# First cross attention of a two-layer Perceiver block: each context turned by 32-row strips in one burst, placed around the scores

## The reference

```python
qp = einsum('bsi,id->bsd', q, kernel_q) + bias_q      # q = layernorm(x)
kp = einsum('bsi,id->bsd', k, kernel_k) + bias_k      # k = v = ctx_1024
vp = einsum('bsi,id->bsd', v, kernel_v) + bias_v
logits = einsum('bqd,bkd->bqk', qp, kp) / sqrt(512) + mask
attn = softmax(logits, axis=-1)
x = x + einsum('bqk,bkd->bqd', attn, vp)
```

## Time and profile before

| | us |
|---|---|
| median of 3 runs | 1436.13 (1433.35 to 1438.67) |
| the profiled execution | 1430.72 |
| its span, first to last instruction | 1429.4 |
| PE busy in the span | 1299.4 (91%) |
| DVE busy | 735.0 (51%) |
| ACT busy | 500.5 (35%) |
| mean granted clock of TensorE | 0.965 of full speed |

### The profile page before, as it was taken

The page is one execution under the profiler, slowest core; times in us unless marked ns, Lnnn a source line. Parts: engine busy times, 40 slices in busy tenths (PEclk is TensorE's granted clock), DMA queues, the critical chain, the costliest instruction groups (busy, mean ns, idle before and its releaser), DMA issues. The chain is left out here.

```text
span 1429.4 us, 25759 instructions
## 1 busy us (share of the span) xinstructions
PE 1299.4 (91%) x11133; PEld 947.5 (66%) x11133; DVE 735.0 (51%) x1501; ACT 500.5 (35%) x977; POOL 148.2 (10%) x153
## 2 busy tenths in 40 slices
PE   6999869989777899999999999998888688999998
PEld 5655554456435677777777777776677556888787
DVE  6367464535698355444555444555772455443442
ACT  3233224322103254544554454542433232221321
POOL 3400030044435000000000000000130100000000
PEclk9999989999988999999999999998999989999999
DMA  9134030000111011000011000002300010000100
GB/s 321 62 118 171 7 118 0 0 1 1 59 67 44 30 33 59 31 31 31 31 33 59 31 32 31 31 2 89 46 0 0 2 66 30 30 30 30 60 30 30
DMA packets 50757, 67.24 MB, mean 47 GB/s; under 512 B 18586, under 2 KB 19660, under 8 KB 50644
## 3 DMA queue, kind: packets, MB, share of 16 engines
q1 hardware_dynamic: 49136, 64.25, 13.8%
q10 hardware_dynamic: 1508, 1.35, 0.4%
HBM read 63.49 MB, written 2.10 MB: 46 GB/s over the span
## 5 line engine op out<-in xcount | busy, mean ns | idle before, releaser
L223 PE MATMUL bank<-xT,wT 128*128 128x512 f32 x576 | 138.9, 394 | 1.8 <-DVE wT L239 1.8
L223 PEld LDWEIGHTS bank<-xT,wT 128*128 128x128 f32 x576 | 108.4, 188 | 27.3 <-issue 2.4
L1560 ACT ACTIVATE W<-W,low 128x512 f32<-128x512 f32 x128 | 90.9, 712 | 64.4 <-DVE low L1479 64.4
L173 POOL TENSOR_TENSOR rstd<-rstd,half_pow 128x1 f32<-128x1 f32 x48 | 28.2, 595 | 757.2 <-DVE rstd L169 696.9
L1479 DVE CUSTOM_DVE_ANT_0 W<-bank,mask 128x512 f32<-128x512 f32 x128 | 80.8, 687 | 49.4 <-PE bank L1369 49.4
L223 PE MATMUL bank<-Wkv,ctxT 128*128 128x512 f32 x432 | 105.2, 396 | 0.0
L1472 DVE COPY XT<-bank 128x256 f32<-128x256 f32 x16 | 6.8, 425 | 191.2 <-PE bank L1390 191.2
L1556 ACT ACTIVATE K<-bank,vecT 128x512 f32<-128x512 f32 x64 | 44.0, 688 | 163.0 <-PE bank L223 163.0
L223 PEld LDWEIGHTS bank<-Wkv,ctxT 128*128 128x128 f32 x432 | 79.2, 188 | 28.9 <-issue 12.2
L223 PE MATMUL bank<-ctxT,Wkv 128*128 128x512 f32 x384 | 94.1, 399 | 3.2 <-DVE ctxT L240 3.2
L223 PE MATMUL bank<-woT,hR 128*128 128x512 f32 x384 | 94.8, 403 | 2.2 <-DVE hR L240 2.2
(11 more groups left out here) (346 smaller groups left out, 2129.3 us busy)
## 6 DMA issues: line engine op xcount, KB each, us to landing
W<-in_ctx_dram SPq DMA_DIRECT2D x26, 1024.0 KB, 5.3
XT<-in_ctx_dram SPq DMA_DIRECT2D x6, 1024.0 KB, 7.6
XT<-in_L_ffn_wi_dram SPq DMA_DIRECT2D x4, 1024.0 KB, 6.3
XT<-in_L_ffn_wo_dram SPq DMA_DIRECT2D x4, 1024.0 KB, 5.1
X<-in_x_dram SPq DMA_DIRECT2D x8, 256.0 KB, 10.9
W<-in_L_attn_Wv_dram SPq DMA_DIRECT2D x2, 1024.0 KB, 8.8
out_dram<-X SPq DMA_DIRECT2D x8, 256.0 KB, 2.9
W<-in_L_xattn_kernel_k_dram SPq DMA_DIRECT2D x1, 1024.0 KB, 7.8
```

The source lines that it names most:

```text
L173: pool.tensor_tensor(rstd[:, g:g + 1], rstd[:, g:g + 1], half_pow[:], ALU.pow).then_inc(rstd_ok.s, 1)
L223: ins = pe.matmul(dst, stationary(x, k), moving(y, k), start=(first and n == 0), stop=(last and n == len(passes) - 1), skip_group_check=True)
L1560: act.activation(PR[:, j, :], PR[:, j, :], ACT.Exp, bias=low[:, j:j + 1], scale=-1.0, accum_out=total[:, j:j + 1]).then_inc(expd.s, 1)
```

## The change

Three things change, all in the first cross attention. First, a context is turned by 64 transposes of 32 rows x 128 columns instead of 16 of 128 x 128: four of them stand side by side on the four 32-row strips of the array, and strip r writes bank r, so one burst fills all four banks. Second, since one burst takes all four banks, each burst waits for all the copies of the burst before it, and each engine empties two banks of each context (VectorE banks 0 and 1, ScalarE banks 2 and 3) with a destination in pieces of 32 columns. Third, the two bursts of the next pair move: that of b = 0 goes to the head of the step, ahead of the probabilities and the scores, that of b = 1 to the place between scores and attend; `result` moves one step later, and the loop gets one step more. The sync engine's list is not touched. `turn_strips` and `strip_of` are the second cross attention's own helpers, made common; there nothing else changes.

```diff
+        def turn_strips(first, src_of):
+            for t in range(4):
+                for k in range(4):
+                    for r in range(4):
+                        strip, to = slice(32 * r, 32 * r + 32), 32 * (4 * t + k)
+                        ins = pe.transpose(bank[:, first + r, to:to + 32], src_of(t, k)[strip, :], ident[strip, strip])
+            return ins
+
+        def strip_of(T, first, r):
+            dst = T.rearrange("f t (k s n) -> f (t k) s n", k=4, s=4)[:, :, r, :]
+            return dst, bank[:, first + r, :].rearrange("f (a n) -> f a n", n=32)
...
-            def context_pe(j, r):
-                c, b = r // 2, r % 2
-                if c == 0:
-                    pe.wait_ge(raw_in[j % 3][b].s, raw_in[j % 3][b](j // 3))
-                if 8 * j + r >= 4:
-                    pe.wait_ge((ctx_a if b else ctx_v).s, (ctx_a if b else ctx_v)((8 * j + r - 4) // 2))
...
-                for k in range(KT):
-                    ins = pe.transpose(bank[:, r % 4, k * P:(k + 1) * P], raws[j % 3][:, b, k, c * P:(c + 1) * P], ident[:])
-                ins.then_inc(ctx_pe.s, 1)
+            def context_pe(j, b):
+                pe.wait_ge(raw_in[j % 3][b].s, raw_in[j % 3][b](j // 3))
+                if 2 * j + b:
+                    pe.wait_ge(ctx_v.s, ctx_v(4 * j + 2 * b - 1))
+                    pe.wait_ge(ctx_a.s, ctx_a(4 * j + 2 * b - 1))
...
+                turn_strips(0, lambda c, k: raws[j % 3][:, b, k, c * P:(c + 1) * P]).then_inc(ctx_pe.s, 1)
...
-                for j in range(PAIRS + 1):
-                    if j:
+                pe.wait_ge(row_a.s, row_a(2))
+                for j in range(PAIRS + 2):
+                    if j + 1 < PAIRS:
+                        context_pe(j + 1, 0)
+                    if j >= 2:
+                        result_pe(j - 2)
+                    if 1 <= j <= PAIRS:
                         probs_pe(j - 1)
                     if j < PAIRS:
                         scores_pe(j)
-                    if j == 0:
-                        pe.wait_ge(row_a.s, row_a(2))
-                    if j:
+                    if j + 1 < PAIRS:
+                        context_pe(j + 1, 1)
+                    if 1 <= j <= PAIRS:
                         attend_pe(j - 1)
-                    if j + 1 < PAIRS:
-                        for r in range(8):
-                            context_pe(j + 1, r)
-                    if j:
-                        result_pe(j - 1)
...
-            def context_v(j, c):
-                dve.wait_ge(ctx_pe.s, ctx_pe(8 * j + 2 * c))
-                dve.tensor_copy(ctxT[j % 2][:, 0, c, :], bank[:, 2 * c % 4, :]).then_inc(ctx_v.s, 1)
+            def context_v(j, b, r):
+                dst, src = strip_of(ctxT[j % 2][:, b, :, :], 0, r)
+                dve.wait_ge(ctx_pe.s, ctx_pe(2 * j + b))
+                dve.tensor_copy(dst, src).then_inc(ctx_v.s, 1)
...
+                    if j + 1 < PAIRS:
+                        for r in range(2):
+                            context_v(j + 1, 0, r)
+                    if j >= 2:
+                        result_v(j - 2)
...
                     if j + 1 < PAIRS:
-                        for c in range(C):
-                            context_v(j + 1, c)
-                    if j:
-                        result_v(j - 1)
+                        for r in range(2):
+                            context_v(j + 1, 1, r)
```

More of the change, by code:

```diff
@@ L390, in query_pe @@
                         lambda h, c: XS[:, h, c, n * 512:(n + 1) * 512], C).then_inc(proj.s, 1)
[L392 to L398 removed]
+            def context_pe(j, b):
[3 more added lines that the diff above has]
+                    pe.wait_ge(ctx_a.s, ctx_a(4 * j + 2 * b - 1))
+                else:
                     pe.wait_ge(wt_v.s, wt_v(3 * C - 1))
[L400 to L402 removed]
+                turn_strips(0, lambda c, k: raws[j % 3][:, b, k, c * P:(c + 1) * P]).then_inc(ctx_pe.s, 1)
             def scores_pe(j):
@@ L406, in scores_pe @@
                     pe.wait_ge(masked.s, masked(j - 1))
+                pe.wait_ge(ctx_v.s, ctx_v(4 * j + 3))
+                pe.wait_ge(ctx_a.s, ctx_a(4 * j + 3))
                 for c in range(C):
-                    pe.wait_ge(ctx_v.s, ctx_v(4 * j + c))
-                    pe.wait_ge(ctx_a.s, ctx_a(4 * j + c))
                     for b in range(2):
@@ L448, in tensor @@
                     rows_pe(2 * m + 1)
-                for r in range(4):
-                    context_pe(0, r)
+                context_pe(0, 0)
                 pe.wait_ge(xt_v.s, xt_v(G - 1))
@@ L453, in tensor @@
                     query_pe(u)
-                for r in range(4, 8):
-                    context_pe(0, r)
+                context_pe(0, 1)
                 for u in range(4, 8):
@@ L545, in vector @@
                     rows_v(g)
-                for c in range(2):
-                    context_v(0, c)
+                for r in range(2):
+                    context_v(0, 0, r)
                 dve.wait_ge(fold_p.s, fold_p(2))
@@ L554, in vector @@
                 dve.tensor_tensor(fold_s[:, 1, :], fold[:, 1, :], fold_s[:, 0, :].bitcast(F32), ALU.subtract).then_inc(fold_v.s, 1)
-                for c in range(2, C):
-                    context_v(0, c)
+                for r in range(2):
+                    context_v(0, 1, r)
                 dve.wait_ge(mask_in.s, mask_in(1))
                 v(dve.tensor_scalar(mask, mask, -1.0, None, ALU.mult))
-                for j in range(PAIRS + 1):
+                for j in range(PAIRS + 2):
+                    if j + 1 < PAIRS:
+                        for r in range(2):
+                            context_v(j + 1, 0, r)
+                    if j >= 2:
+                        result_v(j - 2)
                     if j < PAIRS:
@@ L594, in weight_a, with context_a @@
                 split_a(T[:, 0, c, :], bank[:, u + c, :]).then_inc(wt_a.s, 1)
-            def context_a(j, c):
-                act.wait_ge(ctx_pe.s, ctx_pe(8 * j + 2 * c + 1))
-                act.copy(ctxT[j % 2][:, 1, c, :], bank[:, (2 * c + 1) % 4, :]).then_inc(ctx_a.s, 1)
+            def context_a(j, b, r):
+                dst, src = strip_of(ctxT[j % 2][:, b, :, :], 0, r)
+                act.wait_ge(ctx_pe.s, ctx_pe(2 * j + b))
+                act.copy(dst, src).then_inc(ctx_a.s, 1)
             def query_a(u):
@@ L625, in scalar @@
                         split_a(views[g][0], rows_bank(g)).then_inc(xt_a.s, 1)
-                context_a(0, 0)
-                context_a(0, 1)
+                for r in (2, 3):
+                    context_a(0, 0, r)
                 for u in range(4):
                     query_a(u)
-                context_a(0, 2)
-                context_a(0, 3)
+                for r in (2, 3):
+                    context_a(0, 1, r)
                 for u in range(4, 8):
@@ L640, in scalar @@
                 act.copy(cneg[:], bank[:, 3, 0:PAIRS]).then_inc(row_a.s, 1)
-                for j in range(PAIRS + 1):
+                for j in range(PAIRS + 2):
                     u = j % 2
-                    if j:
+                    if j + 1 < PAIRS:
+                        for r in (2, 3):
+                            context_a(j + 1, 0, r)
+                    if j >= 2:
+                        for b in range(2):
+                            dst, src = attended(0, j - 2, b)
+                            act.wait_ge(ot_pe.s, ot_pe(j - 2))
+                            split_a(dst, src).then_inc(ot_a.s, 1)
+                    if 1 <= j <= PAIRS:
                         act.wait_ge(pt_pe.s, pt_pe(j - 1))
@@ L649, in scalar @@
                                        accum_out=total[:, u:u + 1]).then_inc(expd.s, 1)
-                    if j:
+                    if j + 1 < PAIRS:
+                        for r in (2, 3):
+                            context_a(j + 1, 1, r)
+                    if 1 <= j <= PAIRS:
                         act.wait_ge(av.s, av(j - 1))
                         act.copy(o[:], bank[:, 6, :]).then_inc(av_a.s, 1)
[L653 to L660, removed]
                     if j == C + 1:
@@ L1327, in free_bank @@
                 return bank[:, n % 4, :]
[L1329 to L1337, removed]
             def context_pe(i):
@@ L1344, in context_pe @@
                     pe.wait_ge(q_v.s, q_v(7))
-                turn_strips(lambda c, k: raw[:, k, c * P:(c + 1) * P]).then_inc(ctx_pe.s, 1)
+                turn_strips(4, lambda c, k: raw[:, k, c * P:(c + 1) * P]).then_inc(ctx_pe.s, 1)
             def keys_pe(i, m):
@@ L1380, in probs_pe @@
                     pe.wait_ge(lowest.s, lowest(XPAIRS * i + XPAIRS - 1))
-                turn_strips(lambda t, k: PR[:, j0 + t, k * P:(k + 1) * P]).then_inc(pt_pe.s, 1)
+                turn_strips(4, lambda t, k: PR[:, j0 + t, k * P:(k + 1) * P]).then_inc(pt_pe.s, 1)
             def attend_pe(i):
@@ L1451, in tensor @@
                     output_pe(g, ctxT, 0, C).then_inc(proj.s, 1)
-            def context_strip(i, h, r):
```

(6 more changed lines are left out.)

## The result

The changed kernel takes 1467.59 us, the median of four runs (1465.43 to 1471.34), against 1436.29 before on the same chip: ratio 1.0222, 95% interval 1.0193 to 1.025, so 31 us slower. The forecast was 1465, between 1450 and 1474. The profiled execution is the longest of the four, 1471.34 (span 1470.1), and that of before lay 5.6 under its median, so the two traces differ by 40.6 and the medians by 31.3.

A forecast was written before the change was run, and what follows sets the result against it. The matrix engine was taken to bound the loop, but for a 0.82 us wait. Five steps of 10.23 + 5.5 + 2.3 = 18.0 us plus a slower start gave +28.9, forecast 1465, range 1450 to 1474.

The forecast's parts named there:

- The wait for the transfer: Loop steps j = 2 to 6: the first burst waits 5.5 us for a transfer issued only when attend ends.
- The clock after the stall: Behind each of five stalls: burst, transposes and scores run at a lowered clock, costing 2.3 us more.
- the clock stays low longer: Rival, chance 0.11: another 5.2 us of scores run slow behind each stall, which costs 4.1; +37.7 in all, 1474.
- The first two steps: Loop start: the burst of context 0 of pair 2 idles 3.5 us for VectorE's copies, plus 1.5 for low clock.
- Strip copies at no cost, bursts at 1.12: In the loop: 32-column copies cost the same as dense ones and stay hidden; each burst takes 1.12 us.
- The prologue, left out at ±0.7: Ahead of the loop: second burst saves at most 0.7 us, a new wait for `row_a` takes some back; not counted.
- The sum: Whole kernel: +28.9 us, giving 1459.6 for the profiled execution and 1465 on the median; chance 0.68.
- The rival "faster": Chance 0.04: in the loop the transfers stay hidden and only the shorter turning is left; -10.1 us, 1426.

The follow-up runs named there:

- move-alone run: The changed kernel's places kept, but each burst made of 16 full 128x128 transposes with dense copies; 1475.69 us against 1433.2 for the kernel before, ratio 1.0292.
- the two busy ones: Changed kernel plus 12 or 6 useless matmuls ahead of the burst in the five stalled steps; 1478.61 us with 12, 1453.39 with 6.

## Why the prediction was right, point by point

- **The wait for the transfer** (5.5 a stall, five stalls): measured 5.54, 5.76, 5.63, 5.73 and 5.62 idle. Right in place, number and size; the runs without refills and with one more buffer show that it is the cause.
- **The clock after the stall** (2.3 each, 11.5 in all): the mechanism holds, the size was low. A step takes 18.93 - 10.23 - 5.66 (mean idle) = 3.0 more than its work and its wait, 15 in all; keeping the engine busy gave 3.0 a step back. The term went wrong in how long the clock stays low: 5.2 us were taken from the one restart of the earlier trace rows; behind the five restarts at 99.28, 118.88, 137.08, 156.52 and 174.68 it was 7.3, 4.8, 7.0, 4.6 and 7.0, and the steps lost 3.6, 2.4, 3.5, 2.3 and 3.5. In three of five the rival "the clock stays low longer", with 4.1 a stall, was the truer one. In the move-alone run, which restarts with full transposes (at 100.58, 121.06, 141.11, 161.32 and 181.57), windows read the same way give 5.1, 5.1, 5.6, 5.8 and 6.1. From its fall to its return the clock was low for 10.2, 6.8, 10.2, 6.8 and 10.2 in the changed kernel and for 6.8 each time in that run. That strips prolong it in some steps is therefore likely, but one execution of each was traced and no run was made for it alone.
- **The first two steps**: idle 3.27 against 3.5, right. For the low clock 1.5 were forecast; burst, probabilities and scores behind this wait take 1.7 longer, but in this execution the clock had fallen once more ahead of the first scores, which took 5.24 to the next start for 3.48. In the five other runs whose strips and waits are the same up to here (no refills, the two busy ones, one more buffer, the same with the first context full) the first scores took 3.58 and the second step lost 3.2 to 3.3. So 3.2 to 3.4 in all six: the term was sized at half, and the 1.7 that fits it is luck.
- **Strip copies at no cost, bursts at 1.12**: right.
- **The prologue, left out at ±0.7**: the step that failed, though small. The shorter first burst leaves 2.90 idle ahead of the query products in place of 2.15, the clock falls there, and the products, 11.0 to the next start before, take 12.6 in the changed kernel and up to 13.9 in the other runs with this burst. What the second burst saves is more than eaten; the trace with a full first burst shows it (11.2 behind 2.15), and its median is 2.5 lower (1428.58 against 1431.07).
- **The sum**: between the profiled executions the products behind the loop start at 206.35 against 169.44 (the end of the loop before), so 36.9 later for 28.9 forecast: 4.5 of the difference from the five steps, 1.3 from the later start of the loop, 1.75 from the first scores. Another 3.8 between the two spans lie behind the loop, where nothing was changed. The medians differ by 31.3, which is 9.3 less than the two profiled executions do. That the forecast came within 2.6 of the median is therefore in part luck: in the traces three of its terms were too low, all the same way.
- **The rival "faster"** was the right picture of what the shorter turning is worth without the stall, but 10 us was too much: 1429.7 without refills is 3.5 below before, since the steps of that run take 10.7 to 11.05 where VectorE quantises (its copies come late) and 10.5 where it does not, and not 10.23, and the prologue and the second step lose the clock.

## What to carry to other kernels

When work is moved forward in a list, look at what each of its inputs was set off by: here the transfer had been free only because a whole step lay between its trigger and its reader, and the move put the reader right behind the trigger. A wait on the matrix engine costs more than its length, here 5.6 and 3 more in clock, so price both. A buffer that lets the trigger move by the same step as the reader takes the loss away; a clear gain, 0.3%, came only with the first context turned in full as well.

## What the runs showed of the hardware that I had not expected

- A matmul with 64 output columns takes as long alone as with a partner in the other half: 12 alone took 10.4 (0.87 each), the 8 of scores, in two halves, 3.48 (0.87 a pair). The run with one more buffer keeps the two halves of attend apart by their tiles, and there they start together (each matmul is recorded twice):

```profile
123.58 0.59 PE L452 MATMUL bank<-raw_more,pT 128*64 128x512 f32 x1
123.58 0.59 PE L452 MATMUL bank<-XT,pT 128*64 128x512 f32 x1
124.00 0.59 PE L452 MATMUL bank<-raw_more,pT 128*64 128x512 f32 x1
124.01 0.59 PE L452 MATMUL bank<-XT,pT 128*64 128x512 f32 x1
```

- Four strips side by side turn a context in 1.12 against 1.77 (107.06 to 108.83 in the run with full transposes in the old places), but keep the clock up less well: with 1.43 idle between bursts and 0.56 behind it holds with full transposes, and with 1.44 and at most 0.35 it falls with strips. By the Trainium skill ("TensorE: Matmul & The Clock Gate", section "Part 4: PE-mode transpose") a transpose in TensorE's transpose mode "doesn't count as PE-busy the same way"; its figures are for bf16. For full f32 transposes this trace differs: 40 of them, with 2.0 idle, fill the 6.8 between attend and scores, and the clock stayed at 1.00, where stalls of 5.6 without work brought it to 0.50.
